# Two slots of mask flags, and three of the four low parts of v on GpSimd, in a masked graph-attention kernel

## The reference

```
h        = maximum(layernorm(x), 0)
scores   = h @ weight @ input.T                      # 6144 x 6144
scores   = where(adj > 0, scores, -2**32 + 1)
out      = x + softmax(scores / 0.07, axis=1) @ input
```

## Time and profile before

| | us |
|---|---|
| median of 3 runs | 941.21 (941.16 to 942.68) |
| the profiled execution, whole | 944.59 |
| its span | 942.8 |
| TensorE busy | 919.7 (98%) |
| VectorE busy | 821.4 (87%) |
| ScalarE busy | 756.8 (80%) |
| GpSimd busy | 629.6 (67%) |
| TensorE's mean granted clock | 0.995 of full |

### The profile page before, as it was taken

The page is one execution under the profiler, slowest core; times in us unless marked ns, Lnnn a source line. Parts: engine busy times, 40 slices in busy tenths (PEclk is TensorE's granted clock), DMA queues, the critical chain, the costliest instruction groups (busy, mean ns, idle before and its releaser), DMA issues.

```text
span 942.8 us, 25837 instructions
## 1 busy us (share of the span) xinstructions
PE 919.7 (98%) x7611; PEld 667.4 (71%) x7611; DVE 821.4 (87%) x1674; ACT 756.8 (80%) x1511; POOL 629.6 (67%) x441
## 2 busy tenths in 40 slices
PE   6979999999999999999999999999999999999997
PEld 4347777777777777777777777777777777777776
DVE  5998898888988888888889888898888988888886
ACT  4758888888888888888888888888888888888885
POOL 4896777667766777676677667776766776677610
PEclk9979999999999999999999999999999999999999
DMA  9689999999999999999999999999999999999955
GB/s 316 207 200 226 271 267 272 268 250 273 267 266 262 260 268 265 268 268 263 258 268 270 266 254 264 275 262 267 265 263 262 269 269 268 250 270 268 266 94 98
DMA packets 351977, 239.51 MB, mean 254 GB/s; under 512 B 308816, under 2 KB 333520, under 8 KB 333520
## 3 DMA queue, kind: packets, MB, share of 16 engines
q1 hardware_dynamic: 341936, 234.47, 96.3%
q10 hardware_dynamic: 10016, 4.72, 1.8%
HBM read 160.50 MB, written 3.15 MB: 174 GB/s over the span
## 4 chain that ended last, share of the span: by engine, by line
PE 94%; DVE 3%; DMA 1%; ACT 1%; issue 1%; SPq 0%; DVEq 0%; ACTq 0%
PE ps_s L722 39%; PE ps_o L763 26%; PE ps_t L740 13%; PE ps_o L765 13%; DMA nodes_raw<-in_L_gnn_input_dram 1%; DVE probs L526 1%; DVE v L592 1%; PE ps_t L783 1%; PE ps_s L715 1%; PE ps_s L793 1%; DVE pT_lo L548 0%; DVE split L554 0%; DVE pT_hi L544 0%; ACT ps_t L413 0%; PE ps_o L783 0%
## 5 line engine op out<-in xcount | busy, mean ns | idle before, releaser
L526 DVE CUSTOM_DVE_ANT_0 probs<-ps_s,absent 128x1024 f32<-128x1024 f32 x288 | 351.8, 1222 | 82.2 <-PE ps_s L722 75.1
L357 POOL TENSOR_SCALAR absent<-adj_i 128x2048 bf16<-128x2048 int32 x144 | 274.0, 1903 | 194.3 <-DVE chunk_max L526 177.1
L361 POOL TENSOR_SCALAR absent<-absent 128x2048 bf16<-128x2048 bf16 x144 | 274.5, 1906 | 27.7 <-POOL absent L357 27.7
L445 ACT ACTIVATE pT_hi<-ps_t 128x512 f16<-128x512 f32 x282 | 168.3, 597 | 117.4 <-PE ps_t L740 114.7
L413 ACT ACTIVATE ps_t<-probs,neg_max,exp_scale 128x512 f32<-128x512 f32 x288 | 222.8, 774 | 5.8 <-DVE neg_max L536 4.0
L722 PE MATMUL ps_s<-yT_hi,hT_hi 128*128 128x512 f16 x576 | 219.3, 381 | 0.9 <-DVE chunk_max L526 0.9
L722 PE MATMUL ps_s<-yT_lo,hT_hi 128*128 128x512 f16 x576 | 219.2, 381 | 0.0
L763 PE MATMUL ps_o<-v,pT_hi 128*128 128x256 f16 x1152 | 206.8, 273 | 4.7 <-DVE v L592 3.2
L763 PE MATMUL ps_o<-v,pT_dma 128*128 128x256 f16 x1152 | 206.8, 274 | 0.0
L548 DVE TENSOR_TENSOR pT_lo<-ps_t,pT_hi 128x512 f16<-128x512 f32 x288 | 197.0, 684 | 3.0 <-ACT pT_hi L445 2.8
L765 PE MATMUL ps_o<-v,pT_dma 128*128 128x128 f16 x1152 | 199.1, 220 | 0.0
(11 more groups left out here) (70 smaller groups left out, 595.8 us busy)
## 6 DMA issues: line engine op xcount, KB each, us to landing
adj_i<-in_adj_dram SPq DMA_DIRECT2D x144, 1024.0 KB, 5.2
pT_dma<-split SPq DMA_TRANSPOSE x288, 3.5
x_ln<-in_x_dram SPq DMA_DIRECT2D x48, 64.0 KB, 4.9
x_res<-in_x_dram SPq DMA_DIRECT2D x48, 64.0 KB, 4.8
out_dram<-fin ACTq DMA_DIRECT2D x48, 64.0 KB, 2.9
nodes_raw<-in_L_gnn_input_dram ACTq DMA_DIRECT2D x2, 768.0 KB, 7.1
nodes_raw<-in_L_gnn_input_dram SPq DMA_DIRECT2D x2, 768.0 KB, 10.9
w<-in_L_gnn_weight_dram SPq DMA_DIRECT2D x1, 64.0 KB, 2.7
```

The lines of the kernel that those rows point to most:

```text
L357: nc.gpsimd.tensor_scalar(absent[:, c, :], adj_i[:, c, :], 1.0, 0.0, ALU.min, ALU.max)\
L361: nc.gpsimd.tensor_scalar(absent[:, c, :], absent[:, c, :], -ABSENT, ABSENT, ALU.mult, ALU.add)\
L445: nc.scalar.activation(pT_hi[:, p % BANKS, :], ps_t[k % BANKS][:, :], ACT.Copy).then_inc(hi_done, 1)
L526: nc.vector.tensor_tensor_reduce(out=probs[:, s, j * SCORE:(j + 1) * SCORE], in0=ps_s[j % 2][:, :], in1=absent[:, c, part * SCORE:(part + ...
```

## The change

`absent` gets two slots, one for odd and one for even tiles, so a present pass waits for the mask of two tiles earlier. GpSimd makes the present passes of tile 1 without waiting for masks of tile 0, the first of them before h of tile 2; it makes the second pass only for part 0 of tile 1, and ScalarE makes it for parts 1 and 2, as an Identity activation with scale -2^64 and bias 2^64, behind its last `v_hi`. Then GpSimd makes the low halves of parts 0, 1 and 3 of v, and only then the flags of tile 2 part 0. VectorE keeps part 2 alone, in step 0 where `v_lo(1)` stood. The numbers that `mask` and `product` wait for follow.

```diff
@@ -73,6 +73,9 @@
     SUMS = 9
 
     EARLY = 4
+
+    V_POOL = (0, 1, 3)
+    V_VECTOR = 2
     HEAD = 3
     TAIL = 5
 
@@ -100,7 +103,7 @@
         nodes_raw = sb("nodes_raw", [P, BLOCKS, D], fp32)
         probs = sb("probs", [P, 2, N], fp32)
         adj_i = sb("adj_i", [P, CONVS, CONV], int32)
-        absent = sb("absent", [P, CONVS, CONV], bf16)
+        absent = sb("absent", [P, 2, CONVS, CONV], bf16)
         pT_hi = sb("pT_hi", [P, BANKS, TURN], fp16)
         pT_lo = sb("pT_lo", [P, BANKS, TURN], fp16)
         split = sb("split", [P, BANKS, 2, TURN], fp16)
@@ -116,6 +119,7 @@
         w = sb("w", [P, D], fp32)
         wT = sb("wT", [P, D], fp32)
         minus_half = sb("minus_half", [P, 1], fp32)
+        absent_top = sb("absent_top", [P, 1], fp32)
         stats = sb("stats", [P, 2, 6], fp32)
         mean_var = sb("mean_var", [P, 2, 2], fp32)
         var_eps = sb("var_eps", [P, 2, 1], fp32)
...
@@ -328,6 +334,7 @@
         def _(pool):
             nc.gpsimd.memset(ident[:, :], 0.0).then_inc(ident_zero, 1)
             nc.gpsimd.memset(minus_half[:, :], -0.5).then_inc(half_done, 1)
+            nc.gpsimd.memset(absent_top[:, :], ABSENT).then_inc(top_set, 1)
             pool.wait_ge(ident_zero, 1)
             nc.gpsimd.affine_select(out=ident[:, :], in_=ident[:, :], compare_op=ALU.not_equal, fill=1.0,
                                     base=0, pattern=[[-1, P]], channel_multiplier=1).then_inc(ident_done, 1)
@@ -348,44 +355,57 @@
                 nc.gpsimd.tensor_scalar(h[:, s, :], x_ln[:, s, :], mean_var[:, s, 0:1], rstd[:, s, :],
                                         ALU.subtract, ALU.mult).then_inc(h_done, 1)
 
-            def convert(u, c, free):
+            def present(u, s, c, free):
                 pool.wait_ge(adj_in[c], u * 16 + 16)
                 if free:
 
-                    pool.wait_ge(masked, u * SCORES + (PER_CONV * (c + 1) - SCORES))
+                    pool.wait_ge(masked, u * SCORES + (PER_CONV * (c + 1) - 2 * SCORES))
                 pool.sem_inc(pool_waited, 1)
-                nc.gpsimd.tensor_scalar(absent[:, c, :], adj_i[:, c, :], 1.0, 0.0, ALU.min, ALU.max)\
+                nc.gpsimd.tensor_scalar(absent[:, s, c, :], adj_i[:, c, :], 1.0, 0.0, ALU.min, ALU.max)\
                     .then_inc(present_done, 1)
+
+            def make_absent(u, s, c):
                 pool.wait_ge(present_done, u * CONVS + c + 1)
                 pool.sem_inc(pool_waited, 1)
-                nc.gpsimd.tensor_scalar(absent[:, c, :], absent[:, c, :], -ABSENT, ABSENT, ALU.mult, ALU.add)\
+                nc.gpsimd.tensor_scalar(absent[:, s, c, :], absent[:, s, c, :], -ABSENT, ABSENT, ALU.mult, ALU.add)\
                     .then_inc(absent_done, 1)
+
+            def convert(u, s, c, free):
+                present(u, s, c, free)
+                make_absent(u, s, c)
+
+            def v_lo_pool(n, i):
+
+                blocks = slice(i * PART, (i + 1) * PART)
+                pool.wait_ge(scale_steps, 4)
+                pool.wait_ge(v_hi_done, i + 1)
+                nc.gpsimd.tensor_scalar(nodes_raw[:, blocks, :], nodes_raw[:, blocks, :], scale, 1.0,
+                                        ALU.mult, ALU.mult).then_inc(v_scaled, 1)
+                pool.wait_ge(v_scaled, n + 1)
+                nc.gpsimd.tensor_tensor(v[:, blocks, 1, :], nodes_raw[:, blocks, :], v[:, blocks, 0, :], ALU.subtract)\
+                    .then_inc(v_lo_pool_done, 1)
 
             make_h(0, 0, False)
             make_h(1, 1, False)
             for c in range(CONVS):
-                convert(0, c, False)
+                convert(0, 0, c, False)
+            present(1, 1, 0, False)
             make_h(2, 0, True)
-            for c in range(CONVS):
-                convert(1, c, True)
-            convert(2, 0, True)
-
-            blocks = slice((PARTS - 1) * PART, PARTS * PART)
-            pool.wait_ge(scale_steps, 4)
-            pool.wait_ge(v_hi_done, PARTS)
-            nc.gpsimd.tensor_scalar(nodes_raw[:, blocks, :], nodes_raw[:, blocks, :], scale, 1.0, ALU.mult, ALU.mult)\
-                .then_inc(v_scaled, 1)
-            pool.wait_ge(v_scaled, 1)
-            nc.gpsimd.tensor_tensor(v[:, blocks, 1, :], nodes_raw[:, blocks, :], v[:, blocks, 0, :], ALU.subtract)\
-                .then_inc(v_last_done, 1)
+            for c in range(1, CONVS):
+
+                present(1, 1, c, False)
+            make_absent(1, 1, 0)
+            for n in range(len(V_POOL)):
+                v_lo_pool(n, V_POOL[n])
+            convert(2, 0, 0, True)
 
             def step(t, par, at):
                 if has(at, 2):
-                    convert(t + 2, 1, True)
-                    convert(t + 2, 2, True)
+                    convert(t + 2, par, 1, True)
+                    convert(t + 2, par, 2, True)
                 if has(at, 3):
                     make_h(t + 3, 1 - par, True)
-                    convert(t + 3, 0, True)
+                    convert(t + 3, 1 - par, 0, True)
 
             steps(pool, step)
 
@@ -461,6 +481,11 @@
                                      scale=y_scale).then_inc(y_hi_done, 1)
                 if k >= 5 and k % 2 == 1:
                     v_hi((k - 5) // 2)
+            act.wait_ge(top_set, 1)
+            for c in range(1, CONVS):
+                act.wait_ge(present_done, CONVS + c + 1)
+                nc.scalar.activation(absent[:, 1, c, :], absent[:, 1, c, :], ACT.Identity, bias=absent_top[:, :],
+                                     scale=-ABSENT).then_inc(absent_early_done, 1)
             for g in range(2):
                 exp_d(0, 0, 0, g, g - 4, None)
             for g in range(2):
@@ -519,13 +544,21 @@
                     .then_inc(hT_lo_done, 1)
 
             def mask(u, s, j):
-                dve.wait_ge(absent_done, u * CONVS + (j // PER_CONV + 1))
+                if isinstance(u, int) and u == 0:
+                    dve.wait_ge(absent_done, j // PER_CONV + 1)
+                elif isinstance(u, int) and u == 1 and j < PER_CONV:
+                    dve.wait_ge(absent_done, CONVS + 1)
+                elif isinstance(u, int) and u == 1:
+                    dve.wait_ge(absent_early_done, j // PER_CONV)
+                else:
+
+                    dve.wait_ge(absent_done, u * CONVS + (j // PER_CONV + 2 - CONVS))
                 dve.wait_ge(scores_made, u * SCORES + (j + 1))
                 dve.sem_inc(dve_waited, 1)
                 c, part = j // PER_CONV, j % PER_CONV
                 nc.vector.tensor_tensor_reduce(
                     out=probs[:, s, j * SCORE:(j + 1) * SCORE],
-                    in0=ps_s[j % 2][:, :], in1=absent[:, c, part * SCORE:(part + 1) * SCORE],
+                    in0=ps_s[j % 2][:, :], in1=absent[:, s, c, part * SCORE:(part + 1) * SCORE],
                     scale=1.0, scalar=LOWEST, op0=ALU.subtract, op1=ALU.max,
                     accum_out=chunk_max[:, s, j:j + 1]).then_inc(masked, 1)
 
@@ -672,9 +705,8 @@
                 mask(1, 1, j)
             for g in range(2):
                 lo_d(0, g, g - 4, g + 1)
-            mask(1, 1, 2)
-            v_lo(0)
-            mask(1, 1, 3)
+            for j in range(2, 4):
+                mask(1, 1, j)
 
             def step(t, par, at):
                 nxt = 1 - par
@@ -702,8 +734,8 @@
                                 x_stats(t + 3, nxt)
                             if z == 2:
                                 invert_sum(t, par)
-                            if at == 0 and z < 2:
-                                v_lo(1 + z)
+                            if at == 0 and z == 0:
+                                v_lo(V_VECTOR)
 
             steps(dve, step)
             finish(TILES - 1, (TILES - 1) % 2, True)
@@ -743,10 +775,10 @@
 
             def product(t, par, k, at):
                 if at == 0 and k % PART_TURNS == 0:
-                    if k // PART_TURNS == PARTS - 1:
-                        pe.wait_ge(v_last_done, 1)
+                    if k // PART_TURNS == V_VECTOR:
+                        pe.wait_ge(v_lo_done, 1)
                     else:
-                        pe.wait_ge(v_lo_done, k // PART_TURNS + 1)
+                        pe.wait_ge(v_lo_pool_done, V_POOL.index(k // PART_TURNS) + 1)
                 if k in MULTIPLIED:
                     p = MULTIPLIED.index(k)
                     pe.wait_ge(turn_freed, evac(t, k - 2, at))
```

4 lines of the change are left out of this document (3 added, 1 removed).

## The result

| | median us | range | runs | profiled execution, span |
|---|---|---|---|---|
| before | 942.0 | 941.16 to 945.65 | 12 | 944.59, 942.8 |
| after | 940.58 | 938.91 to 941.26 | 12 | 940.63, 938.8 |

The ratio of the runs is 0.9975, with a 95% interval of 0.9966 to 0.9985: the change makes the kernel faster, by a quarter of a per cent. The forecast, 935.3, asked for 0.6%, and its range ended at 938.3. So the sign was right and the size was not.

What follows compares the result with a forecast made beforehand. TensorE bounds the kernel, busy 919.7 of 942.8 us, so any gain lies in the first 75 us: 2.6 + 3.25 + 1.73 - 1.7 = 5.9 us. Median 941.21 - 5.9 = 935.3 us, range 932.9 to 938.3.

Steps and rivals of the forecast that it cites:

- GpSimd, ScalarE, VectorE, the first hole: Step 0: engine times after the change; TensorE's 3.56 us wait for VectorE's split, ended at 50.60, shrinks to 0.6.
- the gain of 2.6: Step 0: TensorE starts the scores of tile 2 at 56.0 instead of 58.56, 2.6 us earlier.
- The clock's loss stays if the new hole lowers the clock: Step 0, behind the 3.4 us hole before tile 2's scores: the lowered clock again costs 1.7 us.
- The rival with 18%: The clock does not fall at the new hole before tile 2's scores: gain 7.6, 933.6 us; chance 18%.
- SyncE waits for the present pass ... covered by 0.7: Step 0: SyncE waits until 56.3 in front of two transposes whose splits come at 57, covered by 0.7 us.
- The rest ... I cost it at nothing: From step 1 on: the work is the same and TensorE bound, so no cost.
- The median of the runs is 3.4 below the profiled one, and I subtract the same: Whole kernel: the profiled forecast of 938.7 becomes a median of 935.3, from 941.21 less 5.9.
- The rival "slower": Before 52.8 us: VectorE's masks and splits hold each of GpSimd's six v instructions 1.6 longer, 945.0 us; chance 8%.
- the three rivals outside the range: Tile 2's flags late, only 2.6 gained, 938.6 us (8%); later small waits cancel the gain (4%); GpSimd's v held, 945.0 (8%).

Runs made afterwards that it cites:

- before_again: The kernel before, without an edit, run once more for a trace; 942.74 us in its one run.
- small_after: The kernel after, with the adjacency loads of tiles 3 to 5 cut from 2048 to 64 columns a row; 938.63 us, ratio to before 0.9966.
- lock_free: The kernel after, with VectorE's one v moved behind the row maximum; 938.65 us, ratio to before 0.9965.
- sp_both: sp_early, with the first load of tile 3 in step 0 also moved behind the second pair of turns; 939.46 us, ratio to before 0.9975.
- small_before: The kernel before, with the adjacency loads of tiles 3 to 5 cut to 64 columns a row; 941.81 us, ratio to before 1.0003.
- before_win: The kernel before, with VectorE's third v moved ahead of the next tile's statistics; 941.38 us, ratio to before 0.9995.
- sp_early: The kernel after, with tile 2's last adjacency load issued ahead of the first turns; 940.2 us, ratio to before 0.9978.
- v_alone: The kernel before, with only the new division of v (three parts GpSimd, one VectorE), one flag slot; 944.9 us, ratio to before 1.0023.
- flags_alone: The kernel after, with v divided as before (VectorE three parts, GpSimd one), keeping two slots and ScalarE's flags; 939.79 us, ratio to before 0.9978.

## Why the prediction was wrong in size

The times of steps, from the profiled executions, in us:

| | step 0 | step 1 | step 2 | step 3 | step 4 | step 5 | sum |
|---|---|---|---|---|---|---|---|
| before | 30.77 | 18.51 | 18.51 | 18.53 | 18.61 | 18.52 | 123.45 |
| before_again | 27.22 | 18.51 | 18.50 | 18.53 | 18.61 | 18.52 | 119.89 |
| after | 24.34 | 19.44 | 18.50 | 19.82 | 18.61 | 18.86 | 119.57 |
| small_after | 23.07 | 18.52 | 18.51 | 18.53 | 18.61 | 18.59 | 115.83 |

*GpSimd, ScalarE, VectorE, the first hole: right.* The ends of GpSimd's three parts, 43.4, 48.1 and 52.85, the passes of ScalarE, v's end at 54.5, hT_lo and TensorE's start of the scores at 55.97 came as forecast, within some 0.1, and so did the gain of 2.6. The first hole was 0.42, forecast 0.6. The lock between the two engines was behind it: that v which must wait ends 1.6 after GpSimd's instruction was seen in after (54.48) and lock_free (57.4 behind 55.81). The Trainium skill's "SBUF — State Buffer", section "Who interferes with whom", adds that issue order decides who blocks. lock_free, where GpSimd began 0.21 ahead and v took 3.30, and before_again, where v began 0.24 ahead and GpSimd's pass took 3.35, agree; at 0.04 us, in before, the order that the record shows and the outcome do not.

*"The clock's loss stays if the new hole lowers the clock": wrong in the profiled execution of after, for a hole of 3.36.* The rival with 18% held there. In sp_both the clock fell behind a hole of 3.24. One cannot take it as sure from either. By itself this error made the forecast 1.7 too long, and so by luck it hides part of the next one. Nor is this execution the rule: its mean granted clock is 1.00, as in 2 of after's 12 runs, while 7 have 0.998 and 3 have 0.996. One loss of 1.7 us is 0.002 of 938.8, so by this estimate the clock fell once or twice in most runs; where it fell in them, no trace shows.

*"SyncE waits for the present pass ... covered by 0.7" and "The rest ... I cost it at nothing": the first failed step.* The load at 56.26 is issued in time for itself, and the 0.7 is even right: the pair's issue at 56.88 is not late. What failed is that only the time of issue was counted and not what the turns then find in front of them. They land after 7.1 to 7.2 us instead of 3.8; the load issued at 56.26 landed at 63.17 and the turns at 64.08 and 65.56. In step 0 this costs 1.1 us (55.97 to 68.97 are 13.0 us, for 11.9 of work), of which TensorE's two waits for turns show 0.9, and in steps 1, 3 and 5 the later loads do it again: 0.93 + 1.29 + 0.34 = 2.6 us. small_after gives both back, 1.27 and 2.5. The earlier trace rows could not show it, since before, each 1 MB load of step 0 was issued behind a pair of turns; the diff and SyncE's queue could. The Trainium skill says, in "DMA: Bandwidth & Descriptors", section "Two DMAs through the same engine are not ordered", that within one queue of one DMA engine descriptors start in order. The 7.2 against 3.8 us agree with that, though no run here shows the order inside a queue.

For the profiled execution this closes the sum: 938.7 was forecast, + 2.6 in steps 1 to 5, + 1.1 in step 0, - 1.7 for the clock = 940.7, and 940.63 was measured. The 1.1 is what step 0 had left over the forecast's work, so that this term closes by its making; small_after's 1.27 is what confirms it.

*"The median of the runs is 3.4 below the profiled one, and I subtract the same": the second failed step.* The 3.4 were not overhead that both kernels share. They were the third v that lost the race to GpSimd, with the longer hole and the lower clock behind it, and those were just what the sum counted as gained. before_again's step 0 is 3.55 shorter than before's. From the ordinary execution, step 0 gains 27.22 - 24.34 = 2.9 and steps 1 to 5 lose 2.6: 0.3 us on these two. small_before, whose set-up was as quick as after's, agrees: its span is 939.1 against 938.8. The medians differ by 1.4, and the ratio of 0.9975 is 2.4 us. What lies between is not settled. In a group of 24 runs of before 17 are at 941.0 to 942.0. Four are at 943.0 to 943.4, about where before_again lies with its lower clock in the set-up, and three at 944.6 to 947.1, the lowest of them where the profile of before lies, which lost the race; only these three can be laid to it, and that without a trace. The set-up makes its difference in either kernel's variants: in the nine profiles whose clock was 1.00 over 22 to 44 us step 0 begins at 44.4 to 44.7 us, and in the five where it was 0.92 (before_again, before_win, sp_early, lock_free, v_alone) at 46.1 to 46.5.

Of the 5.9 us forecast, then, some 3.5 existed in the profiled execution alone, and 3.7 were given to the queue of DMAs, less the 1.7 of the clock. And the value of moving v was misjudged: flags_alone does as well. The move takes the race at the third v away. The runs of after spread over 2.4 us and those of before over 4.5, which fits this but doesn't show it.

The rival "slower" did not come: GpSimd's subtractions took 3.10 and 3.11 beside VectorE's masks and splits. One slip in the chances changes nothing: the three rivals outside the range had 8, 4 and 8%, which is 20 and not 18.

## What to carry to other kernels

When a change makes one engine earlier or later, write down the order in which the issuing queue then emits its DMAs, and look for a large load that comes just in front of a small transfer that somebody waits for; a queue that issues in time can still double the latency (7.2 against 3.8 us here). Before a gain is read from a profiled execution that is longer than the median, look for what in it the other executions don't have, above all two instructions that hold each other up and start within some tenths of a microsecond. A stretch of work that shows no hole is only safe as long as every wait that borders on it keeps its order.
